# A recommender's interaction kernel: zero-padded 128-row products for tiles 0 to 13, the last tile in units, the top layer of the last two tiles in parts of 160 and 96 columns

## The reference

```python
emb = emb_tables[arange(26)[:, None], x_cat]          # 26 tables of 12500 rows x 64
dense_embed = price[:, None] @ Wp + bp                # one more "field" of 64
feats = concatenate([emb^T, dense_embed])             # [2048, 27, 64]
gram = einsum('bid,bjd->bij', feats, feats)           # all pairs of the 27
interactions = gram[:, upper triangle]                # 351 a row
h = relu(dense_embed @ W1 + b1)                       # 64 -> 128
dense_out = relu(h @ W2 + b2)                         # 128 -> 64
t = relu(concatenate([interactions, dense_out]) @ Wt1 + bt1)   # 415 -> 256
out = (t @ Wt2 + bt2)[:, 0]
```

## Time and profile before

| | |
|---|---|
| time, median of 3 runs | 543.82 us (543.25 to 543.84) |
| profiled execution, its own time | 542.15 us |
| its span, first to last instruction | 540.3 us |
| POOL busy | 393.8 us (73%), 425 instructions |
| PE busy | 246.3 us (46%), 1496 products' records |
| ACT, DVE busy | 169.1 us (31%), 145.4 us (27%) |
| mean granted TensorE clock | 0.70 of 2.4 GHz |

### The profile page before, as it was taken

How to read it: one execution, slowest core, us unless ns; L and a number is a source line. 1 busy time by engine, 2 the same in 40 slices (tenths; PEclk the granted TensorE clock), 3 DMA queues, 4 the chain that set the end, 5 groups by cost and what they waited for, 6 DMA issues and landing times.

```text
span 540.3 us, 4362 instructions
## 1 busy us (share of the span) xinstructions
PE 246.3 (46%) x1496; PEld 177.9 (33%) x1496; DVE 145.4 (27%) x358; ACT 169.1 (31%) x405; POOL 393.8 (73%) x425
## 2 busy tenths in 40 slices
PE   0118033240569515134249733315136960565775
PEld 0105033240534304133234423305134440544654
DVE  3003233040331504123040331503233051333353
ACT  0124323041241604223042440503224052243563
POOL 6777777777777777777777777777777777777750
PEclk9999665555659856555577975755555985669798
DMA  6233333333323333333333333333332333332210
GB/s 187 26 26 27 26 28 27 26 27 27 26 27 27 26 27 28 26 26 27 26 29 26 27 27 26 27 27 27 26 27 26 26 28 26 26 28 27 28 22 2
DMA packets 14360, 16.26 MB, mean 30 GB/s; under 512 B 7169, under 2 KB 7425, under 8 KB 14209
## 3 DMA queue, kind: packets, MB, share of 16 engines
q0 software_dynamic: 13312, 13.66, 30.9%
q1 hardware_dynamic: 578, 2.19, 1.1%
q10 hardware_dynamic: 448, 0.14, 0.1%
HBM read 15.95 MB, written 0.01 MB: 30 GB/s over the span
## 4 chain that ended last, share of the span: by engine, by line
POOL 68%; issue 26%; DMA 2%; PE 2%; ACT 1%; DVE 0%; POOLq 0%
POOL gathered L200 68%; DMA gathered<-in_table,row_idx 2%; PE ps_mlp L487 1%; ACT gram L141 1%; PE ps_trans L419 1%; DMA raw_idx<-in_x_cat 0%; POOLq L50 0%; PE ps_gram L456 0%; PE ps_mlp L479 0%; PE ps_mlp L495 0%; DVE feats L166 0%; DVE top L368 0%; ACT scores L279 0%; DVE row_idx L339 0%; DVE wrapped L332 0%
## 5 line engine op out<-in xcount | busy, mean ns | idle before, releaser
L200 POOL DMA_INDIRECT gathered<-in_table,row_idx x416 | 392.7, 944 | 128.0 <-issue 125.9
L419 PE MATMUL ps_trans<-ident,gathered 128*128 128x128 f32 x208 | 45.4, 381 | 223.0 <-DMA gathered<-in_table,row_idx 223.0
L456 PE MATMUL ps_gram<-feats 64*128 64x128 f32 x1024 | 105.2, 384 | 61.0 <-ACT gram L141 30.2
L141 ACT COPY gram<-ps_gram 32x112 f32<-32x112 f32 (+1 forms) x272 | 97.2, 357 | 108.1 <-PE ps_gram L456 105.2
L141 DVE COPY gram<-ps_gram 32x112 f32<-32x112 f32 (+1 forms) x272 | 96.6, 355 | 116.8 <-PE ps_gram L456 113.5
L456 PEld LDWEIGHTS ps_gram<-feats 64*128 64x128 f32 x1024 | 96.9, 286 | 75.4 <-issue 52.6
L419 PEld LDWEIGHTS ps_trans<-ident,gathered 128*128 128x128 f32 x208 | 35.0, 198 | 236.3 <-issue 234.9
L151 ACT COPY feats<-ps_trans 64x448 f32<-64x448 f32 (+1 forms) x60 | 34.1, 569 | 195.4 <-PE ps_trans L419 195.0
L151 DVE COPY feats<-ps_trans 64x448 f32<-64x448 f32 (+1 forms) x60 | 36.8, 613 | 203.3 <-PE ps_trans L419 202.7
L487 PE MATMUL ps_mlp<-gram,wt1p_sb 128*128 128x512 f32 (+2 forms) x168 | 60.2, 520 | 2.9 <-ACT gram L141 2.9
L487 PEld LDWEIGHTS ps_mlp<-gram,wt1p_sb 128*128 128x128 f32 x168 | 32.6, 228 | 32.6 <-issue 28.0
(11 more groups left out here) (24 smaller groups left out, 33.5 us busy)
## 6 DMA issues: line engine op xcount, KB each, us to landing
gathered<-in_table,row_idx POOLq DMA_INDIRECT x416, 3.3
price_bc<-in_price SPq DMA_DIRECT2D x1, 1024.0 KB, 5.2
wt1p_sb<-in_wt_pairs SPq DMA_DIRECT2D x1, 896.0 KB, 7.8
raw_idx<-in_x_cat SPq DMA_DIRECT2D x1, 195.0 KB, 2.7
w_sb<-in_w ACTq DMA_DIRECT2D x2, 32.0 KB, 4.8
wt1d_sb<-in_wt_dense ACTq DMA_DIRECT2D x1, 64.0 KB, 7.7
raw_idx<-in_x_cat SPq DMA_DIRECT2D x1, 13.0 KB, 1.8
consts_sb<-in_consts ACTq DMA_DIRECT2D x1, 4.5 KB, 2.0
```

Of the source, the lines that this page charges most:

```text
L141: last = copy(gram_to[QUAD * c:QUAD * (c + 1), n % 2, t - BATCHES[n][0], :, rg * r:rg * (r + 1), :, s], source[QUAD * s:QUAD * (s + 1), :, ...
L200: pool.indirect_dma_start(out=gathered[:, to * D:(to + 1) * D], out_offset=None, in_=rows, in_offset=bass.IndirectOffsetOnAxis(ap=row_idx[ ...
L419: last = nc.tensor.transpose(ps_trans[:, to + k * P:to + (k + 1) * P], gathered[:, base + f * D:base + (f + 2) * D], ident[:, :])
L456: last = nc.tensor.matmul(ps_gram[:, out_at:out_at + P], group, group, start=True, stop=True)
```

## The change

- **Tiles 0 to 13.** A new tile `padded` holds `feats` again, with 256 columns for each group: the first 64 partitions' block in columns 0 to 127, the other 64 partitions' in columns 128 to 255, zeros elsewhere (set once by a second memset). ACT fills it with two copies of 64x2048 a tile (`pad_halves`), after the evacuation. A gram round is then 8 products of 128 rows by 256 columns (`gram_round`) where it was 16 of 64 rows by 128 columns.
- **Dense layers.** Four batches of 512 columns, in tiles 0 to 3; `dense_out` now holds the whole batch.
- **Tile 14** keeps 64-row products, in 4 rounds with copies of 32x56 (`fine_round`). Tiles 14 and 15 are one batch.
- **Tile 15** is gathered in four units of 7, 6, 7 and 6 columns. A unit completes 32 batch rows: its transposes, evacuation (`evacuate_unit`; units 0 and 2 also `evacuate_shared` on DVE, for the two fields that a pair of units shares) and one gram round of 4 groups x 2 halves. The row indices of the last tile come from 12 small sums on DVE instead of one; the two iotas of `last_base` on POOL go.
- **Top layer of the last batch** in two parts: 160 columns (tile 14 and unit 0) after unit 0's round, 96 columns (units 1 to 3) at the end, the latter summed in `ps_trans`. Scores are stored and written out in two parts too, the first of 1952 columns.
- **Fillers**: none before unit 1, 6 products before unit 2's transposes, 6 before unit 3's, 4 before the last part of the top layer.

`top_sums`, not shown, is the loop of the old `top_layer` for a given slice; `part_relu`, `store_part` and `score_part` are the old functions for a part.

```diff
-UNITS = 2
-UNIT = HALF // UNITS
+UNITS = 4
+UNIT = P // UNITS
+SIDE = UNIT // 2
+COLS = FIELDS // UNITS
+SHARED = UNITS * COLS
...
-LAST_CHUNKS = [(0, 8), (8, 16), (16, 24), (24, 26)]
-LAST_ROUNDS = 4
-LAST_RG = GROUPS // LAST_ROUNDS
-
-BATCHES = [(0, 4), (4, 8), (8, 12), (12, 14), (14, 15), (15, 16)]
+PAIR = 2 * COLS + 1
+UNIT_COLS = [[PAIR * (n // 2) + (COLS + 1) * (n % 2) + g for g in range(COLS + 1 - n % 2)] for n in range(UNITS)]
+LATE = 3 * UNIT
+EARLY = 2 * P - LATE
+FINE_ROUNDS = UNITS
+FINE_RG = GROUPS // FINE_ROUNDS
+
+BATCHES = [(0, 4), (4, 8), (8, 12), (12, 14), (14, 16)]
+DENSE = BATCH // BANK
 WIDE = 4
 BUFFERS = 1
 
-WARM = (0, 7, 3, 1, 1)
-TO_GRAM, TO_TOP = 4, 5
+WARM = (0, 6, 6, 4)
...
+        def evacuate_unit(copy, n, kk):
+
+            src = ps_trans[D * kk:D * (kk + 1), BANK * (n % 2):BANK * (n % 2) + COLS // 2 * P]
+            src = src.rearrange("p (m q h b) -> p h m q b", m=COLS // 2, q=UNITS, h=2)
+            for h in range(2):
+                dst = feats[D * h:D * (h + 1), SIDE * n:SIDE * (n + 1), 1:1 + SHARED]
+                dst = dst.rearrange("p b (m k q) -> p k m q b", m=COLS // 2, k=2, q=UNITS)
+                last = copy(dst[:, kk], src[:, h])
             return last
+
+        def evacuate_shared(copy, n):
+
+            at = BANK * (n % 2) + COLS // 2 * P
+            src = ps_trans[0:D, at:at + P].rearrange("p (w e h b) -> p h w e b", w=2, e=2, h=2)
+            for h in range(2):
+                dst = feats[D * h:D * (h + 1), SIDE * n:SIDE * (n + 2), SLOTS - 2:SLOTS]
+                last = copy(dst.rearrange("p (w b) e -> p w e b", w=2), src[:, h])
+            return last
+
+        last_batch = batch_of[LAST]
+
+        def last_part(m, late):
+
+            if not late:
+                return slice(0, EARLY), ps_mlp[m][:, 0:EARLY]
+            return slice(EARLY, 2 * P), ps_trans[:, BANK * m:BANK * m + LATE]
...
-            for q in range(2):
-
-                pool.wait_ge(base_made, q + 1)
-                pool.iota(last_base[HALF * q:HALF * (q + 1), :], pattern=[[0, UNITS], [2 * VOCAB, FIELDS // 2]],
-                          base=q * VOCAB, channel_multiplier=0).then_inc(base_made, 1)
-            pool.wait_ge(base_made, 3)
             pool.memset(ident[:, :], 0.0).then_inc(ident_zeroed, 1)
             pool.wait_ge(ident_zeroed, 1)
             pool.affine_select(out=ident[:, :], in_=ident[:, :], compare_op=ALU.not_equal, fill=1.0,
...
+            def pad_halves(t):
+
+                act.wait_ge(trans_evac_dve, NC * (t + 1))
+                act.wait_ge(trans_evac_act, NC * (t + 1))
+                act.wait_ge(dense_slot_set, 2 * (t + 1))
+                for h in range(2):
+                    nc.scalar.copy(padded[D * h:D * (h + 1), :, P * h:P * (h + 1)],
+                                   feats[D * h:D * (h + 1), :, :].rearrange("p (g s) j -> p g (s j)", s=GROUP))\
+                        .then_inc(padded_made, 1)
 
...
             for t in range(LAST):
                 n = batch_of[t]
-                first = t == BATCHES[n][0]
+                first = t == BATCHES[n][0] and n > 0
                 odd_fields(0, t)
+                dense_slots(t)
+                if t < DENSE:
+                    dense_batch(t)
                 if first:
-                    dense_batch(n)
-                dense_slots(t)
-                if first and n > 0:
                     top_relu(n - 1)
                 odd_fields(1, t)
-                if first and n > 0:
+                if t < DENSE:
+                    hidden_relu(t)
+                if t < LAST - 1:
+                    pad_halves(t)
+                if first:
                     store_scores(n - 1)
-                gram_round(0, t)
-                if first:
-                    hidden_relu(n)
-                gram_round(1, t)
-                if first:
-                    dense_out_relu(n)
-
-            t, n = LAST, batch_of[LAST]
-            odd_last(0)
-            dense_batch(n)
+                for r in range(ROUNDS if t < LAST - 1 else FINE_ROUNDS):
+                    gram_round(r, t)
+                if t < DENSE:
+                    dense_out_relu(t)
+
+            t = LAST
+            odd_unit(0)
             dense_slots(t)
-            top_relu(n - 1)
-            odd_last(1)
-            store_scores(n - 1)
-            hidden_relu(n)
-            dense_out_relu(n)
-            for r in range(LAST_ROUNDS // 2):
-                gram_round(r, t)
-            odd_last(2)
-            odd_last(3)
-            for r in range(LAST_ROUNDS // 2, LAST_ROUNDS):
-                gram_round(r, t)
-            top_relu(n)
-            store_scores(n)
+            gram_round(0, t)
+            part_relu(0)
+            odd_unit(1)
+            gram_round(1, t)
+            store_part(0)
+            odd_unit(2)
+            gram_round(2, t)
+            odd_unit(3)
+            gram_round(3, t)
+            part_relu(1)
+            store_part(1)
...
+            for q in range(UNITS):
+                part = slice(UNIT * q, UNIT * (q + 1))
+                to = row_idx[part, b:e].rearrange("p (k c) -> p k c", c=PAIR)
+                from_ = clamped[part, b:e].rearrange("p (k c) -> p k c", c=PAIR)
+                base = field_base[part, 0:SHARED].rearrange("p (o g q) -> p q o g", o=1, q=UNITS)[:, q]
+                for c in (0, COLS + 1):
+                    nc.vector.tensor_tensor(to[:, :, c:c + COLS], from_[:, :, c:c + COLS],
+                                            base.to_broadcast([UNIT, 2, COLS]), ALU.add).then_inc(rows_made, 1)
+                nc.vector.tensor_tensor(to[:, :, COLS], from_[:, :, COLS],
+                                        field_base[part, SHARED + q % 2:SHARED + q % 2 + 1].to_broadcast([UNIT, 2]),
+                                        ALU.add).then_inc(rows_made, 1)
             nc.vector.memset(feats[:, :, :], 0.0).then_inc(feats_zeroed, 1)
-            dve.wait_ge(feats_zeroed, 1)
+            nc.vector.memset(padded[:, :, :], 0.0).then_inc(feats_zeroed, 1)
+            dve.wait_ge(feats_zeroed, 2)
...
+            def transpose_unit(n):
+
+                wait_trans_evac(NC * LAST + max(n - 1, 0))
+                keep_warm(n, n % 2)
+                pe.wait_ge(unit_gathered[n], 16 * len(UNIT_COLS[n]))
+                base = (LAST % BUFFERS) * ROW
+                for m in range(COLS // 2):
+                    at, to = base + UNIT_COLS[n][2 * m] * D, BANK * (n % 2) + m * P
+                    last = nc.tensor.transpose(ps_trans[:, to:to + P], gathered[:, at:at + 2 * D], ident[:, :])
+                if n % 2 == 0:
+                    at, to = base + UNIT_COLS[n][COLS] * D, BANK * (n % 2) + COLS // 2 * P
+                    last = nc.tensor.transpose(ps_trans[0:D, to:to + P], gathered[:, at:at + D], ident[:, :])
+                last.then_inc(unit_transposed, 1)
+
...
+            def gram_round(t, r):
+                pe.wait_ge(padded_made, 2 * (t + 1))
+                wait_gram_evac(ROUNDS * t + r)
+                for g in range(RG):
+                    at = RG * r + g
+                    last = nc.tensor.matmul(ps_gram[:, 2 * P * g:2 * P * (g + 1)], feats[:, GROUP * at:GROUP * (at + 1), :],
+                                            padded[:, at, :], start=True, stop=True)
+                last.then_inc(gram_done, 1)
+
+            def fine_round(t, r):
+                if t == LAST:
+                    wait_trans_evac(NC * LAST + r + 1)
+                else:
+                    wait_trans_evac(NC * (t + 1))
+                pe.wait_ge(dense_slot_set, 2 * (t + 1))
+                wait_gram_evac(rounds_before(t) + (max(r - 1, 0) if t < LAST else r - 1))
+                for g in range(FINE_RG):
+                    for h in range(2):
+                        at = (FINE_RG * r + g) * GROUP
+                        group = feats[D * h:D * (h + 1), at:at + GROUP, :].rearrange("p s j -> p (s j)")
+                        to = 2 * BANK * (r % 2) + h * BANK + g * P
+                        last = nc.tensor.matmul(ps_gram[:, to:to + P], group, group, start=True, stop=True)
+                last.then_inc(gram_done, 1)
...
+            def top_part(m, late):
+
+                if not late:
+                    pe.wait_ge(score_stored, last_batch)
+                top_sums(last_batch, m, *last_part(m, late), rounds_before(LAST) + (FINE_ROUNDS if late else 1))
...
             for t in range(LAST):
                 n = batch_of[t]
-                first = t == BATCHES[n][0]
+                first = t == BATCHES[n][0] and n > 0
                 transpose_chunk(t, 0)
-                if first and n > 0:
+                if first:
                     top_layer(n - 1)
                 transpose_chunk(t, 1)
-                if first and n > 0:
+                if t < DENSE:
+                    hidden_layer(t)
+                if first:
                     score(n - 1)
-                gram_round(t, 0)
-                if first:
```

(43 more changed lines are left out.)

250 lines of the change are left out of this document (129 added, 121 removed).

## The result

The changed kernel takes 544.50 us (median of 20 executions, 543.37 to 548.42); the kernel before takes 542.05 (median of 20, 540.22 to 544.18). The ratio is 1.0056 with a 95% interval of 1.0037 to 1.0076: slower by half a per cent, 2.45 us in the medians. The ratio is one of means, which differ by 3.1 us (545.31 against 542.25). The forecast was +2.4 us. Its own median, 546.2, is 1.7 us too high, since it was built on the three-run median of 543.82, which lies near the top of what 20 executions of that kernel give. The profiled execution of the changed kernel took 544.48, its span is 542.7.

What follows compares the result with a forecast made beforehand. POOL's gathers, one per 1.249 us, were taken as the bound, plus a 15.6 us tail. The last top layer starting 3.2 us later and running 0.8 shorter gave +2.4: span 542.7, median 546.2, range 541.8 to 549.

Steps and rivals of the forecast that it cites:

- slip of tile 14's second transposes: Behind tile 13's heavier work and a 256-column top layer, these transposes come 0 to 0.5 us later; 0.2 taken.
- tile 14's copies end: Tile 14's four gram rounds go back to back, their copies taking 8.65 us, until 505.15.
- early top layer: After unit 0's round, from 510.7: 32 records, 14 at low and 18 at high clock, some 7.0 us.
- unit 2's transposes: In the last tile: landed at 517.2, unit 2 waits for six fillers that end at 523.65.
- unit 3's transposes: In the last tile: landed at 524.7, unit 3 waits for fillers until 529.7; the step trusted most.
- late top layer: At the end: starts at 534.75 against 531.56 before, and takes 4.7 us against 5.5.
- The mechanism: In the tail, PE comes 5 us late to the last landing, behind early top layer and 5.6 us of fillers.
- 160 columns: Price of one record in the early top layer: 0.17 us at the high clock, 0.29 at the low.
- Padding, dense batches, start: Start and tiles 0 to 13: no effect unless a deadline is missed; pads 2.0 us, rounds 3.8 to 7.2.
- The stall: Rival: POOL waits up to 3 us at each of tiles 4, 8 and 12, giving 549 to 556; chance 0.08.
- the start of the first top layer: In tile 4: heavier tile 3 delays it about 3 us, leaving 3 us before POOL's deadline of 198.5.
- The on-time rival: In the tail: PE passes unit 3's fillers by the landing at 524.8, 2.5 us less, 541.3; chance 0.22.

Runs made afterwards that it cites:

- e4: Changed kernel without fillers before units 2 and 3, early top-layer halves moved behind units 1 and 2 on PE: 539.03 us, 0.9952 of before.
- e9: Changed kernel with 64-row products and no padded copies in tiles 0 to 13, without fillers before units 2 and 3: 543.65 us, 1.0033 of before.
- e10: Changed kernel with 64-row products in tiles 0 to 13 and the last batch's top layer whole at the end: 543.13 us, 1.0034 of before.
- e12: Changed kernel with 64-row products in tiles 0 to 13, plus eight fillers after unit 0's transposes and three after its round: 541.12 us, 0.9995.
- e2: Changed kernel with 64-row products and no padded copies in tiles 0 to 13: 544.82 us, 1.0048 of before.
- e1: Changed kernel without the six fillers before unit 2 and the six before unit 3: 543.26 us, 1.0027 of before.
- e3: Changed kernel, padding kept, plus eight fillers after unit 0's transposes and three after its round: 542.29 us, 1.0001 of before.
- e8: Changed kernel, padding kept, with the last batch's top layer whole at the end: 545.45 us, 1.0033 of before.
- e5: Changed kernel with e4's reordered tail, 64-row products and no padded copies in tiles 0 to 13: 538.24 us, 0.9922 of before.
- e6: Kernel before plus only the padded copies and 128-row products in tiles 0 to 13: 543.66 us, 1.0015 of before.
- e7: e5 plus eight fillers after unit 0's transposes and four after unit 1's: 538.16 us, 0.9922 of before.
- e11: e5 without its last four fillers, so with none at all: 540.62 us, 0.9986 of before.

## Why the prediction was right, step by step

| step, start in us | forecast | after |
|---|---|---|
| last gather | 521.92 | 521.94 |
| slip of tile 14's second transposes | 0.2 | 0.65 |
| tile 14's copies end | 505.15 | 505.49 |
| early top layer | 510.7 | 512.22 |
| its length | 7.0 | 7.0 |
| unit 2's transposes | 523.65 | 525.06 |
| unit 3's transposes | 529.7 | 531.04 |
| late top layer | 534.75 | 536.16 |
| its length | 4.7 | 3.9 |
| from there to the span's end | 3.2 | 2.6 |
| span | 542.7 | 542.7 |

- **The mechanism** was the one forecast: fillers and early top layer ahead of the units in PE's order. e4 shows it by moving them, e9, e10 and e12 by taking one thing at a time. In the profiles the fillers alone are worth 1.2 us of the span (e9 against e2), the early part 1.7 (e10 against e2), and the half clock ahead of unit 1 some 3.2 (e12 against e2). These are prices of single steps and need not add up.
- **That the sum came out to a tenth is luck**, twice. In the profiled execution two errors cancel (next point). And the medians agree because the changed kernel's lies at the top of its lower group: by the means the change costs 3.1 us, with the 9 slowest executions in it, and without those 9 the mean would be 1.7 us over before.
- **Two terms were mis-sized and cancelled.** The early top layer started 1.5 us late. Unit 0's round ran at the half clock after PE's idle 4.4 us, 0.9 us more; the forecast priced only the top layer itself for that clock. Of the rest, 0.3 is tile 14's slip and 0.2 the evacuation between. At the other end, a record of 96 columns took 126 ns (1.77 / 14), not the 155 of a 128-column one, so 0.8 us less; and 0.6 came from the end of the kernel, where the first half of the score no longer waits for DVE's relu (one product pair of 0.33 us is left behind it instead of 0.60) and 1.48 us pass after the last store is issued instead of 1.78.
- **160 columns** took 290 ns a record at the half clock, as forecast, and 155 ns at the high clock, as 128 did, where 170 was forecast. 14 records at the half clock and the rest high was right too.
- **Padding, dense batches, start**: nothing in the profiled execution. The pad copies and rounds came close to the forecast prices (1.89 us for 2.0; 3.7 and 6.7 us for 3.8 and 7.2). The Trainium skill (TensorE: Matmul & The Clock Gate, Part 3: Packing small matmuls) says that small products can run side by side in the array; the trace agrees: at the full clock the 32 records of a packed round took 2.06 us, the 16 of a padded one 3.69. Packing them again (e2) gained nothing in the median, as it is a loss off the chain.
- **The stall** was given 0.08 and up to 3 us at each of three places. The traces show it at one place, 2.0 to 4.0 us: POOL idle 1.97, 2.79 and 4.04 us at the 157th gather in the profiles of e1, e3 and e8. By the upper groups of the times it comes in 27 of 56 executions of the padded kernels with early dense batches (after, e3, e4, e8; e1 is not counted, as its groups overlap) and in 1 of 42 of their packed twins (e2, e5, e10, e12). That the executions above the gap are the stalled ones is inferred from these pairs and the profiles, since no trace of each execution exists: the profiled executions of e3 and e8 are in the upper groups and have the stall, those of after and e4 are in the lower ones and have none. A gap alone would prove little. The times of the kernel before, without any padding, have groups too (540.2 to 541.1, 541.9 to 542.1 and 543.3 to 544.2), and one execution each of the packed e2 and e9 is over 3 us above all others of its kernel (548.41, 547.42); no run explains these.
- **The step of the forecast that missed the stall** is the start of the first top layer. It let the heavier tile 3 delay it by 3 us; its sums started 4.5 us later than before in the changed kernel's profile (161.61 against 157.07) and 8.2 later in e8's (165.25). With tile 4's rounds starting at 181.1, as forecast, even e8's two slow rounds would have met the deadline (181.1 + 6.52 + 3.26 + 6.73 = 197.6). The forecast had called the dense batches free in tiles with slack; tile 3's was not (2.6 us, under e6). The stall belonged into the sum as nearly an even chance of 2 to 4 us.
- **The on-time rival** needed PE to gain 4.9 us. In e12 the late top layer started 3.8 us earlier than in the changed kernel, and it came to 0.9995 of before; e4 gained 6.6 and e5 5.0, mostly by the order, and came to the other side. Its price was 2.5 us under before; e4 and e5 measured 3.0 and 4.6.

The best version is e5 (or e7): 0.9922, 4.6 us under the kernel before. It keeps the change's units, the split and the dense batches, drops the padding and the fillers ahead of units 2 and 3, and spreads the early top layer over the gaps.

## What to carry to other kernels

Splitting the last tile into smaller units shortens the steps behind the last landing only if the in-order engine is free at that landing: walk along that engine's program with real prices, and put useful work, not fillers, into the gaps between landings. Filler products can be worth something inside a wait (3 us in e12, 2 in e5 against e11, nothing that could be measured in e7). Outside one they stand on the chain, even if part of it comes back through the clock (5.6 us of fillers, 1.2 us net in e9). An engine with half its time idle can still be late at one place; for extra work that is "hidden", find the deadline at which a buffer must be free, and sum up to it at the lower clock, from the tile before on.
